# Transformer block on one core: int4-style weights dequantised by GpSimd beside the attention instead of beside the projection, and the loads of these pieces moved to SyncE

## What is computed

```
x = x + attention(layernorm(x))      # 32 heads of 16, causal, softmax; q, k, v, o projections with bias
x = x + ffn(layernorm(x))            # 512 -> 1792 -> 512, gated; its weights are quantised
x = x + topk_mlp(layernorm(x))       # 512 -> 1376 -> 512
x = x + ffn(layernorm(x))            # the same quantised weights again
weight = (int_weight - zero[group]) * scale[group]      # groups of 128 rows
```

## Time and profile before

| | |
|---|---|
| median of 3 runs | 2164.5 us (2162.3 to 2167.2) |
| the profiled execution | 2164.9 us, its span 2163.1 us |
| busy in the span | TensorE 2014.5 us (93%), VectorE 1565.1 (72%), ScalarE 1020.2 (47%), GpSimd 560.5 (26%) |
| projection | 0 to 187.7 us |
| attention | 187.7 to 770.4 us |
| output, MLP | 770.4 to 831.0, 831.0 to 2163.1 us |

### The profile page before, as it was taken

The page is one execution under the profiler, slowest core; times in us unless marked ns, Lnnn a source line. Parts: engine busy times, 40 slices in busy tenths (PEclk is TensorE's granted clock), DMA queues, the critical chain, the costliest instruction groups (busy, mean ns, idle before and its releaser), DMA issues. The chain is left out here.

```text
span 2163.1 us, 38405 instructions
## 1 busy us (share of the span) xinstructions
PE 2014.5 (93%) x14288; PEld 1236.3 (57%) x14288; DVE 1565.1 (72%) x2736; ACT 1020.2 (47%) x1658; POOL 560.5 (26%) x587
## 2 busy tenths in 40 slices
PE   5887999999999977899999999999999999999989
PEld 2342344444444344677667667666666666666756
DVE  6775677777777432169888988978889889788941
ACT  3221356565655621156366454553664545535511
POOL 2223453842523332111210311212103112121221
PEclk9997799999999988999999999999999999999999
DMA  7766235432333164020222013013130130131000
GB/s 258 234 214 176 70 95 137 126 86 68 93 95 83 33 196 167 9 98 1 87 72 100 6 53 120 6 53 119 59 125 1 54 115 1 53 115 53 11 11 11
DMA packets 115656, 187.35 MB, mean 87 GB/s; under 512 B 43200, under 2 KB 68176, under 8 KB 115520
## 3 DMA queue, kind: packets, MB, share of 16 engines
q1 hardware_dynamic: 91344, 133.22, 19.9%
q0 software_dynamic: 9088, 32.12, 5.3%
q10 hardware_dynamic: 15088, 20.19, 2.7%
HBM read 151.59 MB, written 33.62 MB: 86 GB/s over the span
## 5 line engine op out<-in xcount | busy, mean ns | idle before, releaser
L842 DVE TENSOR_REDUCE mx<-s 128x1 f32<-128x512 f32 (+3 forms) x608 | 380.9, 660 | 128.8 <-PE s L731 75.0
L823 ACT ACTIVATE pr<-s 128x1024 f32<-128x1024 f32 (+3 forms) x352 | 300.7, 868 | 243.8 <-PE s L750 181.7
L1467 ACT ACTIVATE kept<-ax,T 128x1376 f16<-128x1376 f32 x248 | 357.0, 1439 | 122.0 <-DVE T L1541 116.1
L1535 DVE TENSOR_SCALAR_CACHE_REDUCE junk<-ax,T 128x1376 f16<-128x1376 f32 x248 | 406.5, 1639 | 3.1 <-DVE T L1528 0.5
L1326 POOL TENSOR_TENSOR lohi<-h,lohi 128x256 f16<-128x256 f32 x224 | 173.6, 775 | 872.9 <-ACT lohi L1478 872.7
L1364 PE MATMUL ga<-xT_f,w_gate 128*128 128x256 f16 x2688 | 332.7, 274 | 7.9 <-DVE h L1592 4.9
L1374 PE MATMUL acc<-w_down,lohi 128*128 128x512 f16 x1344 | 326.3, 379 | 8.7 <-POOL lohi L1326 8.7
L1364 PE MATMUL ub<-xT_f,w_up 128*128 128x256 f16 x2688 | 331.6, 273 | 0.0
L1364 PEld LDWEIGHTS ga<-xT_f,w_gate 128*128 128x128 f16 x2688 | 263.3, 98 | 79.9 <-DVE h L1592 7.5
L1364 PEld LDWEIGHTS ub<-xT_f,w_up 128*128 128x128 f16 x2688 | 263.9, 98 | 31.2
L728 PE MATMUL s<-K,Q 65*128 65x512 f16 (+3 forms) x768 | 245.2, 345 | 26.3 <-DMA K<-onerow 13.5
(11 more groups left out here) (142 smaller groups left out, 2352.5 us busy)
## 6 DMA issues: line engine op xcount, KB each, us to landing
ring<-wgu_scr SPq DMA_DIRECT2D x64, 688.0 KB, 5.3
ring<-wd_scr SPq DMA_DIRECT2D x24, 768.0 KB, 4.7
wgu_scr<-tk_h POOLq DMA_DIRECT2D x16, 344.0 KB, 6.0
q_scr<-qk_h ACTq DMA_DIRECT2D x16, 256.0 KB, 4.0
k_scr<-qk_h ACTq DMA_DIRECT2D x16, 256.0 KB, 2.5
v_scr<-v_f ACTq DMA_DIRECT2D x16, 256.0 KB, 2.9
Q<-q_scr SPq DMA_DIRECT2D x32, 128.0 KB
K<-k_scr SPq DMA_DIRECT2D x32, 128.0 KB
```

Of the source, the lines that this page charges most:

```text
L823: nc.scalar.activation(pr[:, kb % 2, j0:j1, 0:w], scores, ACT.Exp, scale=SCALE).then_inc(e2_ok, 1)
L842: nc.vector.tensor_reduce(dst, s1[u % 2][:, 0:(j1 - j0) * w].rearrange("p (j k) -> p j k", k=w), AX.X, ALU.max).then_inc(r1_ok, 1)
L1467: nc.scalar.activation(kept[0][:, :], ax[k % 2][:, 1, :], ACT.Sign, scale=-1.0, bias=TF[:, 1:2], accum_out=cnt[:, 1:2]).then_inc(c1_ok, 1)
L1535: nc.vector.tensor_scalar(junk[:, :], ax[k % 2][:, 0, :], TF[:, 0:1], -float(KZERO), ALU.is_lt, ALU.add, accum_out=cnt[:, 0:1]).then_inc(c ...
```

## The change

Projection: nothing is dequantised there. ScalarE makes the high half of q, k itself, with a second activation from PSUM, in place of VectorE's cast. `qk_h`, `v_f` and the transposes' PSUM tiles have four buffers instead of two. SyncE issues the stores, and all of x. The three weight matrices have buffers of their own, the first is loaded and split in four parts. The sum before the root of the variance goes from GpSimd to VectorE.

Attention: GpSimd dequantises all three matrices in 46 pieces (32 of 448 columns, 14 of 512), five operations each, spread over the 16 quads by `dq_slot`. Two buffers hold a piece's inputs, so piece m can be loaded when piece m - 2 is done: `dq_load` puts its load at the quad in which piece m - 2 is worked on. SyncE issues all loads of pieces, also those of the top-k layer, in `load_pieces(n)`, behind `store(n)`. The multiplication by 1024 has a second operand (times 1.0) where it had none. SyncE's and GpSimd's loops over quads are written out. TensorE's, VectorE's and ScalarE's part of the attention stays as it is.

```
-            pool: for n in range(NQ): beside_ones(n, ...); load_down / split_down; split_weights(m) ...
+        dq_slot = [m * NQ // NDQ for m in range(NDQ)]                    # NDQ = 46, NQ = 16
+        dq_load = [dq_slot[m - 2] if m >= 2 else -1 for m in range(NDQ)]
+        tk_slot = [m * NQ // NTK for m in range(NTK)]                    # NTK = 19
+        tk_load = [tk_slot[m - 2] if m >= 2 else -1 for m in range(NTK)]
...
+            def load_pieces(n):
+                for m in range(NDQ):
+                    if dq_load[m] == n:
+                        width, wsrc, zsrc, ssrc, _dst = dq_pieces[m]
+                        wait(sp, dq_lo, m - 1)
+                        for dst, src in ((dq_w, wsrc), (dq_z, zsrc), (dq_s, ssrc)):
+                            sp.dma_start(dst[:, m % 2, 0:width], src).then_inc(dq_in[m % 2], 16)
+                for m in range(NTK):
+                    if tk_load[m] == n:
+                        rows, width, src, _stores = tk_pieces[m]
+                        wait(sp, tk_lo, m - 1)
+                        sp.dma_start(tk_raw[0:rows, m % 2, 0:width], src).then_inc(tk_in[m % 2], 16)
...
+            load_pieces(-1)
+            maxima_row(0)
+            for n in range(NQ):
+                if n + 2 < NQ:
+                    load_qk(n + 2, 0)
+                if n + 1 < NQ:
+                    maxima_row(n + 1)
+                if n + 2 < NQ:
+                    load_qk(n + 2, 1)
+                    load_v(n + 2)
+                store(n)
+                load_pieces(n)
...
-                nc.gpsimd.tensor_scalar(raw, raw, WS, None, ALU.mult).then_inc(tk_up, 1)
+                nc.gpsimd.tensor_scalar(raw, raw, WS, 1.0, ALU.mult, ALU.mult).then_inc(tk_up, 1)
...
+            def dequantise(m):
+                width, _w, _z, _s, (hi, lo) = dq_pieces[m]
+                value, raw, zero, scale = (t[:, m % 2, 0:width] for t in (dq_f, dq_w, dq_z, dq_s))
+                pool.wait_ge(dq_in[m % 2], 48 * (m // 2 + 1))
+                nc.gpsimd.tensor_tensor(raw, raw, zero, ALU.subtract).then_inc(dq_sub, 1)
+                pool.wait_ge(dq_sub, m + 1)
+                nc.gpsimd.tensor_scalar(value, raw, WS, 1.0, ALU.mult, ALU.mult).then_inc(dq_up, 1)
+                pool.wait_ge(dq_up, m + 1)
+                nc.gpsimd.tensor_tensor(value, value, scale, ALU.mult).then_inc(dq_mul, 1)
+                pool.wait_ge(dq_mul, m + 1)
+                nc.gpsimd.tensor_copy(hi, value).then_inc(dq_hi, 1)
+                pool.wait_ge(dq_hi, m + 1)
+                nc.gpsimd.tensor_tensor(lo, value, hi, ALU.subtract).then_inc(dq_lo, 1)
 
             for n in range(NQ):
+                beside_ones(n)
+                for m in range(NDQ):
+                    if dq_slot[m] == n:
+                        dequantise(m)
+                for m in range(NTK):
+                    if tk_slot[m] == n:
+                        split_weights(m)
...
# projection, ScalarE (a slot of q or k)
                     act.wait_ge(mm_ok, s + 1)
-                    wait(act, qkl_ok, QK_SLOTS * c + u - 1)
-                    nc.scalar.activation(qk_f[:, u % 2, :], pmm[u % 4][:, :], ACT.Identity, ...).then_inc(qkf_ok, 1)
+                    wait(act, qkl_ok, v - 1)
+                    nc.scalar.activation(qk_f[:, u % 2, :], pmm[u % 4][:, :], ACT.Identity, bias=bias, ...)
+                    wait(act, qk_st[u % NST], 16 * (v // NST))
+                    nc.scalar.activation(qk_h[:, u % NST, 0, :], pmm[u % 4][:, :], ACT.Identity, bias=bias, ...
+                                         ).then_inc(qkf_ok, 1)
# projection, VectorE
-                    wait(dve, qk_st[u % 2], 16 * (v // 2))
-                    nc.vector.tensor_copy(qk_h[:, u % 2, 0, :], qk_f[:, u % 2, :]).then_inc(qkh_ok, 1)
-                    dve.wait_ge(qkh_ok, v + 1)
-                    nc.vector.tensor_tensor(qk_h[:, u % 2, 1, :], qk_f[:, u % 2, :], qk_h[:, u % 2, 0, :], ALU.subtract
+                    nc.vector.tensor_tensor(qk_h[:, u % NST, 1, :], qk_f[:, u % 2, :], qk_h[:, u % NST, 0, :], ALU.subtract
-                if s - 2 in piece_at:
-                    piece_lo(piece_at[s - 2])
-                if s in piece_at:
-                    piece_mul(piece_at[s])
```

More of the change, by code:

```diff
@@ L184, in phase_project @@
-        NPIECE = len(pieces)
+        qk_st = [sem(f"qk_st{i}") for i in range(NST)]
+        v_st = [sem(f"v_st{i}") for i in range(NST)]
         SLOTS = NCH * SPC
-        slot_of = [2 + n * (SLOTS - 5) // NPIECE for n in range(NPIECE)]
-        piece_at = {s: n for n, s in enumerate(slot_of)}
-        assert len(piece_at) == NPIECE and slot_of[-1] + 2 < SLOTS
         RSTD_AT, XN_AT = 2, 4
         block = ctx.enter_context(nc.Block())
[L194 to L198, removed]
@@ L224, in _ @@
+            for i in range(NST):
+                sp.wait_ge(qk_st[i], 16 * QK_SLOTS // NST * NCH)
+                sp.wait_ge(v_st[i], 16 * TPC // NST * NCH)
         @block.gpsimd
@@ L231, in _, with root @@
             pool.wait_ge(id_ok, 2)
[L233 to L238, removed]
-                                        ).then_inc(rs_ok, 1)
-            rstd_chunk(0)
-            for s in range(SLOTS):
-                if s in piece_at:
[L244 to L250, removed]
+            def root(n, t0, t1):
+                pool.wait_ge(ve_ok, n)
+                nc.gpsimd.tensor_tensor(rstd[:, t0:t1], rstd[:, t0:t1], neghalf[:, 0:1].broadcast_to([P, t1 - t0]), ALU.pow
+                                        ).then_inc(rs_ok, 1)
+            root(1, 0, 2)
+            root(2, 2, TPC)
+            for c in range(1, NCH):
+                root(c + 2, 0, TPC)
         @block.scalar
@@ L303, in _ @@
                     xt_hi(c + 1, t)
[L304 to L309, removed]
         @block.vector
@@ L366, in _ @@
+            for t in range(2):
+                normalise(0, t)
+            for t in range(2):
+                xt_lo(0, t)
+                normalise(0, t + 2)
+            first_weight_lo(0)
+            first_weight_lo(1)
+            for t in range(2, TPC):
+                xt_lo(0, t)
+            first_weight_lo(2)
+            first_weight_lo(3)
             dve.wait_ge(b_in, 48)
             nc.vector.tensor_scalar(bias_qk[:, :, :], bias_raw[:, :, :], QS, None, ALU.mult).then_inc(b_ok, 1)
-            weight_lo(1)
@@ L369, in _ @@
-            weight_lo(2)
             for s in range(SLOTS):
@@ L594, in store @@
-            def store(n, h, i):
-                b, g = n // GPB, n % GPB
-                wait_held(sp, regs, (no_ok, n + 1))
-                o = o_scr[bass.ds(b * L, L), bass.ds(g * QR, QR)].rearrange("(n p) d -> p n d", p=P)
-                sp.dma_start(o, o_st[i][:, :, :].rearrange("p (n j) d -> p n (j d)", n=NB)).then_inc(o_out[i], 16)
-            for i in range(2):
-                for f in range(2):
-                    load_qk(i, 0, i, f)
-                load_v(i, 0, i)
-            maxima_row(0, 0)
@@ L606, in slot @@
-            def slot(n, h, i):
-                load_qk(n + 2, h + 1, i, 0)
-                maxima_row(n + 1, 1 - i)
-                load_qk(n + 2, h + 1, i, 1)
-                load_v(n + 2, h + 1, i)
-                store(n, h, i)
-            slot(0, 0, 0)
-            with sp.Fori(0, (NQ - 4) // 2) as t:
-                slot(2 * t + 1, t, 1)
-                slot(2 * t + 2, t + 1, 0)
-            slot(NQ - 3, NQ // 2 - 2, 1)
-            maxima_row(NQ - 1, 1)
-            store(NQ - 2, NQ // 2 - 1, 0)
@@ new lines, in _ @@
+            for n in range(2):
+                for f in range(2):
+                    load_qk(n, f)
+                load_v(n)
+            load_pieces(-1)
[10 more added lines that the diff above has]
+                load_pieces(n)
```

300 lines of the change are left out of this document (128 added, 172 removed).

## The result

The changed kernel takes 2509.2 us (median of 4 runs, 2503.9 to 2518.3) where the kernel before takes 2163.5: a ratio of 1.158 (95% interval 1.154 to 1.162). It is slower by 345.7 us. The forecast was 2448 us, 61 less than measured; the time lies in its range of 2350 to 2540.

A forecast was written before the change was run, and what follows sets the result against it. TensorE was taken to set the attention's pace and to lose time in the projection waiting for `xn`. 2164.9 - 33.1 (projection) + 260 (stalls) + 56 (lower clock) = 2448 us, range 2350 to 2540.

The forecast's parts named there:

- The projection: Projection stage: TensorE runs without waits for `xn`, last product near 151 us; gain 33.1 us, bounds 25 and 38.
- The 2.8 us more for the first six slots: Projection start: 2.8 us added because the first slot runs on the lower clock.
- The chain: Attention: division, store, load of piece a + 2, its operations, top-k pieces, `beside_ones`, then TensorE; 14 stalls, none in slot 8.
- Rival A: Attention: the loads and GpSimd's work are hidden, only the projection's gain is left; 2132 us, chance 0.06.
- The sum of the stalls: Attention: TensorE's 14 waits for `Va`, 14.5 to 29 us each, 260 us together.
- The landing: Attention: piece a + 2 takes 4.6 us from first load issue to first use, bounds 3.1 and 6.2.
- lower bound of 38 us less: Attention stalls: GpSimd's multiplication by 1024 at the cast's pace would take off 38 us; taken as unchanged, 2.55 ns an element.
- the prediction's own last sign: Attention: the forecast would be wrong if the multiplication by 1024 takes another time than 2.55 ns an element.
- The clock: Attention: 8 us at the lower clock after each of 14 stalls, costing 4 each; 56 us, bounds 28 and 98.
- rival C: Attention stalls dearer: multiplication twice as long (+62), landing 6.2 us (+22), clock 7 us a stall (+42); above 2540, chance 0.07.
- rival B: Attention stalls much smaller: fast multiplication, landing 3.1 us, clock back at once; 2250 to 2360 us, chance 0.09.
- Rival D: Projection gains nothing because its loads or stores bound it; 2481 us, inside the range, no chance of its own.

The follow-up runs named there:

- V first: Changed kernel with GpSimd copying V beside ones for the next quad ahead of this quad's pieces: 2165.1 us, 0.997 of the kernel before.
- loads by GpSimd: Changed kernel with GpSimd, not SyncE, issuing the loads of quantised piece m + 2 right behind piece m: 2160.5 us, 0.994 of the kernel before.
- V first with top-k loads by GpSimd: V first, with the top-k pieces' loads issued by GpSimd again and the quantised ones still by SyncE: 2156.0 us, 0.993 of the kernel before.
- the spread: V first with top-k loads by GpSimd, plus quantised pieces over quads 0 to 14 and top-k ones over 1 to 14: 2148.3 us, 0.990 of the kernel before.
- the filled kernel: Changed kernel with unused matmuls in TensorE's 14 waits for `Va` and its slot loop written out: 2414.9 us in the profiled execution.

## Why the prediction was right, point by point

**The projection.** 33.1 us forecast, 35.8 measured. The first product started at 14.87 us, not 16.5, which is 1.6 of the 2.7 more. The 2.8 us more for the first six slots came to 1.6 (72 matmuls in 17.32 us, 15.70 without waits), which is the rest. The reason given for them, a lower clock, is not what the profile says: it has a granted clock of 1.00 from 14 to 30 us in the kernel before, though no more matmuls start there (6 from 22 to 24) than at 0.50 (6 from 44 to 46). That stays open. Of the forecast "no wait for `xn`" 0.9 us behind the first product are left. Which parts pay was not in the forecast: 26.6 us come with the dequantisation alone, 4.2 with the four buffers, and at most 0.4 with the cast moved to ScalarE. The other 5 were not tried one by one.

**The chain.** It was right in place and count: load of piece a + 2 behind the store, 14 waits, none in slot 8. The runs show it from both ends: with V ahead of the pieces, or with the loads out of SyncE's order, all 242.5 us are gone. Rival A, the chain hidden, is out. With it falls the rule of the Trainium skill, DMA: Bandwidth & Descriptors, Issuing engines are not separate DMA queues, as a guide to this case. The same loads cost 349 us more on SyncE's queue than on GpSimd's (2509.2 against 2160.5, on two chips; 1.158 and 0.994 of the kernel before). That section counts only the time of issuing; what decided is what the issuing engine waits for in front of them.

**The sum of the stalls.** 260 us forecast, 242.5 measured, and two of its terms were off in opposite directions. The landing was put at 4.6 us and is 6.5 on the mean, 14 times 1.9, so 26 us were missing. There the step that failed is the reading of the earlier trace rows: its 6.2 us for twice the bytes were taken as an upper bound for one piece. The multiplication by 1024, whose lower bound of 38 us less was stated and not taken, came out there; 39.8 is its price in the waits. By the prediction's own last sign it was wrong here: the multiplication does not take 2.55 ns an element, with a second operand it takes 0.97 (1.34 us for 1376). 260 + 26 - 38 is 248; the other 6 us, 0.4 a wait, are left over.

**The clock.** This is the mis-sized term. 56 us were forecast, bounds 28 and 98. What the attention lost beyond its waits is 379.4 - 242.5 = 136.9 us. The stage's rows show it without this difference: the same 4240 matmuls are busy 687.8 us where they were 543.5, 144.3 more, at a granted clock of 0.69 for 0.95, and TensorE's idle time grew by 235.1, 7.4 less than the waits for `Va`. The forecast had 8 us at 1.2 GHz behind each wait, read from a return after a wait of 6 us; the row that had shown a slow one, 11 us in slot 0, was not given weight. The windows behind the wait that ends at 327.3 and behind the one that ends at 595.1 show both kinds, in the busy time by window of the changed kernel:

```profile
331.00:335.00 4.00, 4.00 (x15) 1.00 (x15) 1.46 (x3) 1.23 (x2) 3.77 (x5) 0.50 0.01 4
355.00:359.00 4.00, 4.00 (x25) 1.39 (x23) 1.43 (x3) 1.73 (x2) 0.00 (x0) 0.50 0.44 124
359.00:363.00 4.00, 3.98 (x28) 1.36 (x25) 2.62 (x4) 1.83 (x2) 0.00 (x0) 0.94 0.05 12
595.00:599.00 4.00, 3.94 (x18) 1.01 (x22) 0.92 (x2) 0.47 (x1) 3.68 (x5) 0.57 0.25 83
599.00:603.00 4.00, 3.87 (x33) 1.64 (x29) 3.24 (x6) 2.66 (x4) 3.77 (x5) 1.00 0.00 0
```

After the first, 2.4 GHz comes back only at 359, 32 us later, with TensorE busy all the time; after the second within 4. From the first product to the next division (L812) the first slot takes 43.8 us (327.34 to 371.09), the second 31.4 (595.06 to 626.41): a slow return costs about 12 us more than a quick one. Nine of the 14 waits have a return of 27 to 32 us, five of 3 to 18. Nine times 12.4 is 112 of the 136.9. Filling the waits took 95 us away, so for these it is shown that TensorE's idleness brought them; the other 42 can lie in the 92 us at the lower clock that stayed there.

**In sum.** -33.1, +260, +56 became -35.8, +242.5, +136.9 and 2.3 in the stages behind: 345.9 by the profiles. Of rival C's three parts the landing and the clock came, and of rival B's the fast multiplication, so the total stayed between them. That it lies inside the range owes something to this: the clock alone was 81 us over its forecast and beyond its own bound of 98. Rival D fell with the projection's gain.

**What was not foreseen.** With the chain cut, the projection's gain did not come back whole: V first is 0.3% faster than the kernel before, where 35.8 us are 1.6%. Its attention is 34.5 us longer than that of the kernel before, and 3.6 without the dequantisation. 10 of the 34.5 are the clock's late return at the stage's start, which comes and goes with the same attention code. Another 12.2 are TensorE's waits for `Q<-zrow`; where these went, rows of maxima were late, 11 to 12 us in each of the loads by GpSimd, V first with top-k loads by GpSimd, and the spread. The other 12, with the clock behind such waits, were not taken apart. Rival A's 2132 us had priced all of this at nothing.

## What to carry to other kernels

Where a load is moved to another engine's queue, write down what stands in front of it there, and when that is released in the consumer's time, not only how long the load takes. A lead of a whole slot vanishes if one buffer's refill is tied to the end of the slot, and all that stands behind it on the consumer's queue, even work that was ready, comes late with it; here it was enough to put the copy that TensorE waits for ahead of the work that nobody waits for. A wait of the busiest engine can be dearer than its length: beside the 242.5 us of waits the attention lost another 136.9, and 95 of them went away when TensorE was kept busy in the waits.

## What the runs showed of the hardware

The lower clock outlasted its cause: behind the wait that ended at 327.3 TensorE ran at 1.2 GHz for 32 us, busy 4.00 of 4.00 us from 331 on, then changed. Behind other waits of the same kind and of 14 to 26 us it was back within 3 to 18. What decides between them was not settled, nor why the clock fell once in the filled kernel with no single wait over 0.7 us in the 5 us before.

GpSimd's multiplication by a constant takes 1.33 us with one operation and 0.56 with two (times 1.0) on 448 elements, 3.68 and 1.34 on 1376: with the second operation it runs at the pace of a cast (1.33 at 1376).
